# An attention and expert kernel on one core: output norms of the turn behind the sigmoid, the third G product in step 13, another order in head and tail

## What is computed

```python
qkv = x @ Wqkv + bqkv
q, k, v = split(qkv, 3)
q, k = q - mean(q), k - mean(k)
q2 = l2norm(q*q / (sum(q*q) + 1e-7), axis=channels)
k2 = l2norm(k*k / (sum(k*k) + 1e-7), axis=tokens)
kv = einsum('bnc,bnd->bcd', k2, v)
x1 = layernorm(x + (v + (q2 @ kv) / sqrt(N)) @ Wln + bln)
sel = sigmoid(x1 @ expert_sel.T)                # 16 experts
scores = relu(einsum('bsd,edh->bseh', x1, keys))
out = layernorm(x1 + einsum('bseh,ehv,bse->bsv', scores, values, sel))
```

## Time and profile before

| | us |
|---|---|
| median of 3 runs | 1004.82 |
| lowest and highest run | 1003.86 and 1009.28 |
| the profiled execution's own time | 1005.64 |
| its span in the profile | 1003.7 |
| TensorE, VectorE, ScalarE, GpSimd busy in it | 984.6, 804.1, 527.2, 54.7 |

### The profile page before, as it was taken

How to read it: one execution, slowest core, us unless ns; L and a number is a source line. 1 busy time by engine, 2 the same in 40 slices (tenths; PEclk the granted TensorE clock), 3 DMA queues, 4 the chain that set the end, 5 groups by cost and what they waited for, 6 DMA issues and landing times.

```text
span 1003.7 us, 20862 instructions
## 1 busy us (share of the span) xinstructions
PE 984.6 (98%) x7704; PEld 942.0 (94%) x7704; DVE 804.1 (80%) x1873; ACT 527.2 (53%) x1151; POOL 54.7 (5%) x75
## 2 busy tenths in 40 slices
PE   9999999999999999999999999999999999999996
PEld 8798998999999999999999999999999999999996
DVE  6799886988778887788878888788877888878545
ACT  5557535565345653556435664366644566354323
POOL 0100100001010010100101000010100101010100
PEclk9999999999999999999999999999999999999999
DMA  5152233432354223441243613325133342333221
GB/s 187 48 201 90 76 106 114 136 122 82 99 159 138 75 87 125 140 153 70 92 135 104 189 55 113 121 96 179 65 107 110 107 164 75 107 105 108 85 95 64
DMA packets 75768, 112.45 MB, mean 112 GB/s; under 512 B 7186, under 2 KB 37906, under 8 KB 75668
## 3 DMA queue, kind: packets, MB, share of 16 engines
q1 hardware_dynamic: 75668, 111.13, 33.9%
HBM read 87.51 MB, written 23.46 MB: 111 GB/s over the span
## 4 chain that ended last, share of the span: by engine, by line
PE 71%; DVE 11%; DMA 5%; issue 5%; ACT 3%; SPq 2%; POOL 0%; DVEq 0%; ACTq 0%; POOLq 0%
PE up_bank L1399 25%; PE down_bank L1399 25%; PE ring_bank L1399 9%; PE qk_bank L1399 6%; PE g_bank L1399 3%; DMA sel_all<-sel_out 3%; DVE gated_l L1137 2%; SPq L478 2%; DMA parked_x<-w_room 2%; DVE gated L1155 2%; DVE x1T_l L1001 1%; PE g_bank L1452 1%; ACT L666 1%; DMA parked_q<-w_room 1%; DVE qk L1155 1%
## 5 line engine op out<-in xcount | busy, mean ns | idle before, releaser
L1399 PE MATMUL down_bank<-vals_h,gated_h 128*128 128x256 f32 x1024 | 285.9, 279 | 1.9 <-DVE gated_l L1137 1.8
L1399 PE MATMUL down_bank<-vals_h,gated_l 128*128 128x256 f32 x1024 | 283.8, 277 | 0.0
L1399 PE MATMUL down_bank<-vals_l,gated_h 128*128 128x256 f32 x1024 | 283.8, 277 | 0.0
L1399 PE MATMUL up_bank<-x1T_h,keys_l 128*128 128x256 f32 (+1 forms) x928 | 268.6, 289 | 0.0
L1399 PE MATMUL up_bank<-x1T_l,keys_h 128*128 128x256 f32 (+1 forms) x928 | 268.6, 289 | 0.0
L1399 PE MATMUL up_bank<-x1T_h,keys_h 128*128 128x256 f32 (+1 forms) x928 | 268.5, 289 | 0.0
L598 ACT ACTIVATE gated_h<-gated 128x512 fp32r<-128x512 f32 x176 | 111.1, 631 | 198.9 <-DVE gated L1155 198.9
L1399 PEld LDWEIGHTS down_bank<-vals_h,gated_h 128*128 128x128 f32 x1024 | 192.4, 188 | 8.0 <-DVE gated_l L1137 3.6
L1399 PEld LDWEIGHTS down_bank<-vals_l,gated_h 128*128 128x128 f32 x1024 | 192.9, 188 | 4.1
L1399 PEld LDWEIGHTS down_bank<-vals_h,gated_l 128*128 128x128 f32 x1024 | 192.3, 188 | 0.0
L1155 DVE SCALAR_TENSOR_TENSOR gated<-up_bank,sel_all 128x512 f32<-128x512 f32 x176 | 121.3, 689 | 78.3 <-PE up_bank L1399 55.9
(11 more groups left out here) (276 smaller groups left out, 1772.5 us busy)
## 6 DMA issues: line engine op xcount, KB each, us to landing
sel_all<-sel_out SPq DMA_DIRECT2D x192, 256.0 KB, 3.8
x_raw<-in_x SPq DMA_DIRECT2D x15, 512.0 KB, 5.2
out<-z SPq DMA_DIRECT2D x30, 256.0 KB, 2.5
xT_raw<-in_xT SPq DMA_DIRECT2D x14, 512.0 KB, 5.3
parked_q<-w_room SPq DMA_DIRECT2D x14, 512.0 KB, 2.6
q<-parked_q SPq DMA_DIRECT2D x56, 128.0 KB, 3.0
parked_x<-w_room SPq DMA_DIRECT2D x14, 512.0 KB, 3.8
w_room<-parked_x SPq DMA_DIRECT2D x56, 128.0 KB, 3.0
```

What stands on the lines that cost most here:

```text
L1399: last = mm(dst, lhs, rhs, start=start and i == 0, stop=stop and i == n - 1, **kw)
```

## The change

In the loop:

- GG 2 (the third G product) goes from step 12 to step 13, ahead of GG 3, in the first iteration too.
- On ScalarE the sigmoid of a group (`early` of LG) goes from ahead of the copy gated_h to behind it, in every step that has one (13 and 31).
- The output norms of ZN 29 and ZN 30 are both made in step 31, behind the sigmoid (`norm_steps`); a sigmoid of one column behind z_std in step 30 takes the table load there. Their two stores go to step 31, behind `move_rows`.
- `low_is_late` is false for step 31: gated_l of step 31 is made in its own step, not behind the gate of step 0.

In the head: VectorE's `weights_lo(0)` goes ahead of the column sums, `weights_lo(1)` behind the sum of the logits; TensorE gets 4 and 3 extra fp32 matmuls of 128 columns ahead of the last x1 transposes and ahead of the logits (`keep_warm`).

In the tail: ScalarE norms one tile of each of the last two pairs, VectorE the other; ScalarE's norm stands ahead of the next z_std; each tile has its own store.

```diff
--- before.py
+++ after.py
@@ -41,7 +41,7 @@
         1: [], 2: [("ZA", 0), ("ZA", 1), ("Y", 4)], 3: [("ZN", 0), ("XS", 4)], 4: [("ZN", 1), ("Y", 5)],
         5: [("Y", 6), ("XS", 5)], 6: [("Y", 7), ("XS", 6)], 7: [("XS", 7), ("QK", 0)], 8: [("QK", 1)],
         9: [("GG", 0)], 10: [("XR", 1), ("QK", 2), ("GG", 1)], 11: [("QK", 3), ("QS", 0)],
-        12: [("GG", 2), ("QK", 4), ("LG", 1), ("QS", 1)], 13: [("GG", 3), ("QS", 2)], 14: [("QK", 5), ("QS", 3)],
+        12: [("QK", 4), ("LG", 1), ("QS", 1)], 13: [("GG", 2), ("GG", 3), ("QS", 2)], 14: [("QK", 5), ("QS", 3)],
         15: [("GG", 4), ("QK", 6), ("QS", 4)], 16: [("GG", 5), ("QS", 5)], 17: [("QK", 7)],
         18: [("ZA", 0), ("ZA", 1), ("QR", 0), ("GG", 6)], 19: [("KS", 0), ("GG", 7), ("QS", 6)], 20: [("KV", 0), ("QS", 7)],
         21: [("Y", 0)], 22: [("Y", 1), ("XS", 0)], 23: [("Y", 2), ("XS", 1)], 24: [("Y", 3), ("XS", 2)],
@@ -57,7 +57,7 @@
     0: [], 1: [], 2: [], 3: [("QT", 2)], 4: [("QT", 3)], 5: [("Y", 4)], 6: [("Y", 5)],
     7: [("Y", 6), ("XT", 4), ("QK", 0)], 8: [("Y", 7), ("XT", 5), ("QK", 1)], 9: [("XT", 6), ("GG", 0)],
     10: [("XT", 7), ("QK", 2), ("GG", 1)], 11: [("QK", 3), ("QS", 0)],
-    12: [("GG", 2), ("QK", 4), ("LG", 1), ("QS", 1)]}
+    12: [("QK", 4), ("LG", 1), ("QS", 1)]}
 FIRST = dict(LOOP, plan={**LOOP["plan"], **FIRST_PLAN}, split_xT={4: 0, 9: 1})
 LAST = dict(plan={1: [("ZA", 0), ("ZN", 0)], 2: [("ZA", 1), ("ZN", 1)]}, split_xT={}, split_x={}, bias_x={},
             gpsimd_xT=(), gpsimd_x=())
@@ -351,13 +351,17 @@
             for s in range(LAST_STEPS):
                 step(B, s)
 
+        def norm_steps(s):
+
+            return {STEPS - 2: (), STEPS - 1: (STEPS - 3, STEPS - 2)}.get(s, (s - 1,))
+
         def gate_room(s):
 
             return qk if s % 2 and s not in range(6, 19) else gated
 
         def low_is_late(it, s):
 
-            return gate_room(s) is not gate_room((s + 1) % STEPS) and (it, s) != (B - 1, STEPS - 1)
+            return gate_room(s) is not gate_room((s + 1) % STEPS) and s != STEPS - 1
 
         def last_iteration(it):
             return it == B
@@ -452,11 +456,11 @@
                 g = goff % G
                 b = it + (goff - g) // G
                 t = GT * g + 2 * p
-                if last_iteration(it) and p == 1:
-
-                    sp.wait_ge(last_out_made, 1)
+                if last_iteration(it):
+
+                    sp.wait_ge(last_out_made, p + 1)
                     sp.dma_start(out_dram[b, :, t + 1], z_room(it)[:, p, 1]).then_inc(stored[p], 16)
-                    sp.wait_ge(out_made, 2 * out_pair(it, goff, p) - 1)
+                    sp.wait_ge(out_made, 2 * out_pair(it, goff, -1) + p + 1)
                     sp.dma_start(out_dram[b, :, t], z_room(it)[:, p, 0]).then_inc(stored[p], 16)
                 else:
                     at_least(sp, out_made, 2 * out_pair(it, goff, p))
@@ -549,16 +553,17 @@
                 for kind, a, off in planned(it, s, ("LG", "ZN", "QS", "XS")):
                     if kind == "LG" and a == 0:
                         move_rows(it, off, a)
-                    elif kind == "ZN":
-                        store_pair(it, off, a)
                     elif kind in ("QS", "XS") and a % GT == GT - 1:
                         turn(it, it + off, kind, a // GT)
                 if s == ROWS_STEP and it < B:
                     move_rows(it, 0, 1)
+                for n in norm_steps(s + 1) if s < STEPS - 2 else norm_steps(s):
+                    for kind, a, off in planned(it, n, ("ZN",)):
+                        store_pair(it, off, a)
 
             run(step)
             for p in range(2):
-                sp.wait_ge(stored[p], 16 * (G * B + p))
+                sp.wait_ge(stored[p], 16 * (G * B + 1))
 
 
         @block.gpsimd
@@ -734,22 +739,34 @@
                         act.wait_ge(z_aggregated, 2 * n)
                         nc.scalar.activation(z_std[:, a], z_mv[:, a, :, 1], ACT.Sqrt,
                                              bias=eps_ln[:]).then_inc(z_rooted, 1)
-                for kind, a, off in planned(it, s - 1, ("ZN",)):
+                if s == STEPS - 2 and planned(it, s, ("LG",)):
+                    nc.scalar.activation(table_ahead[:, 1:2], eps_ln[:], ACT.Sigmoid)
+                for n in norm_steps(s):
+                    if not last_iteration(it):
+                        output_norms(it, n)
+
+            def output_norms(it, n):
+
+                for kind, a, off in planned(it, n, ("ZN",)):
                     n = out_pair(it, off, a)
                     act.wait_ge(z_shift_made, n)
-                    for i in range(1 if last_iteration(it) and a == 1 else 2):
-                        nc.scalar.activation(z_room(it)[:, a, i], z_room(it)[:, a, i], ACT.Identity, bias=z_shift[:, a, i:i + 1],
+                    for i in range(1 if last_iteration(it) else 2):
+                        nc.scalar.activation(z_room(it)[:, a, i], z_room(it)[:, a, i], ACT.Identity,
+                                             bias=z_shift[:, a, i:i + 1],
                                              scale=z_rstd[:, a, i:i + 1]).then_inc(out_made, 1)
 
             def step(it, s):
-                early(it, s, ("KS", "LG"))
+                early(it, s, ("KS",))
                 if step_exists(it, s):
                     f = step_no(it, s)
                     act.wait_ge(gate_applied, f + 1)
 
                     at_least(act, down_made, f + 1 - HELD)
                     copy(gated_h[:, f % HELD], gate_room(s)[:]).then_inc(gated_hi, 1)
+                early(it, s, ("LG",))
                 early(it, s, ("QK", "Y"))
+                if last_iteration(it):
+                    output_norms(it, s - 1)
                 late(it, s)
                 if (it, s) == (0, 0):
                     q0_squares(3)
@@ -1016,7 +1033,7 @@
                         V.scalar_tensor_tensor(out=z_shift[:, a], in0=z_mv[:, a, :, 0], scalar=-1.0,
                                                in1=z_rstd[:, a], op0=ALU.mult, op1=ALU.mult
                                                ).then_inc(z_shift_made, 1)
-                        if last_iteration(it) and a == 1:
+                        if last_iteration(it):
                             layer_norm(z_room(it)[:, a, 1], z_room(it)[:, a, 1], z_mv[:, a, 1],
                                        z_rstd[:, a, 1:2]).then_inc(last_out_made, 1)
 
@@ -1334,6 +1351,7 @@
                 dve.wait_ge(bln_in, 16)
                 V.tensor_tensor(out_bias[:], bvl[:], bln_raw, ALU.add).then_inc(out_bias_set, 1)
                 x0_bias(0)
+                weights_lo(0)
                 dve.wait_ge(cols0_summed, 1)
                 V.tensor_scalar(col_sums[:, 0:M].rearrange("p a b -> p (a b)"), cols0_place[:, 0:2 * M],
                                 EPS_NORM ** 2, None, ALU.max)
@@ -1369,12 +1387,11 @@
                     x1T_low(a)
                 for a in range(2):
                     y_finish(2 + a)
-                weights_lo(0)
                 for a in range(2):
                     x1T_low(2 + a)
-                weights_lo(1)
                 dve.wait_ge(logits_low, 1)
                 V.tensor_tensor(sel[:], logits0_bank[0:E, :], sel[:], ALU.add).then_inc(logits_summed, 1)
+                weights_lo(1)
                 for m in range(M):
                     dve.wait_ge(kv_hi, m + 1)
                     V.tensor_tensor(kvw_l[:, m], kvw0[:, m], kvw_h[:, m].bitcast(F32),
@@ -1538,6 +1555,11 @@
                         last = mm(logits0_bank[:], esel_h[:, m], x1T_l[:, 0, m], start=False,
                                   stop=(m == M - 1))
                     last.then_inc(logits_made, 1)
+
+                def keep_warm(count):
+
+                    for n in range(count):
+                        mm(down_bank[0][:, 0:P], ones[:], ident[:], start=True, stop=True)
 
                 pe.wait_ge(constants_set, 4)
                 for n in range(WARM):
@@ -1574,8 +1596,10 @@
                 x1_transpose(0)
                 x1_transpose(1)
                 queries0(2)
+                keep_warm(4)
                 x1_transpose(2)
                 x1_transpose(3)
+                keep_warm(3)
                 logits0()
 
             first_batch()
```

## The result

The changed kernel takes 1014.2 us (median; its runs lie between 1011.2 and 1019.9), against 1006.2 us of the kernel before beside it: ratio 1.0079, 95% interval [1.0052, 1.0107], slower by some 8 us. The forecast was 1009.0 with a range up to 1011.8. The profiled execution of the changed kernel is its longest, 1019.9 us of its own time and 1017.9 of span, so its difference of 14.1 us in the span is more than the typical one; about 5 us of that are a slower pace of the matmuls, told of at the end.

What follows compares the result with a forecast made beforehand. TensorE, busy 984.6 of 1003.7 us, bounds it; VectorE and ScalarE set its step-20 KV wait. 1005.6 + 6.2 - 1.9 + 0.1 - 0.4 = 1009.6; from the runs' median 1008.8, stated as 1009.0, range 1000.8 to 1011.8.

Steps and rivals of the forecast that it cites:

- Part 1: Step 13: sigmoid behind the gate's copy makes k_h 1.50 us later, then GpSimd, gate of step 17 and KV; 6.2 us lost.
- term of 6.2 us: Loss summed over seven KV products from the later gate of step 17: 5.6 plus 0.6 for colliding spreads.
- One sign: Step 20: TensorE's wait ahead of each KV product was to be 1 us.
- My last sign: Step 17: if its gate waits for GpSimd no oftener than before, Part 1 is wrong and the kernel no slower.
- Rival A: Steps 14 to 17: the spread doesn't wait for step 14's transpose, or slack absorbs 1.5 us; about 1002, chance 0.19.
- upper bound of 10.5 us: Most that Part 1 could lose, if nothing takes the delay up: 7 x 1.5 us.
- Part 2: Third G product from step 12 to 13: gain 0, at most 2 us if Part 1 costs nothing.
- Part 3: Turn of a batch: gated_l of step 31 no longer behind gate(0), so TensorE does not wait; 1.9 us gained.
- wait for z in step 2 of a turn: Turn: a small new wait for the z additions was to come next, limiting a turn's gain to 0.44 us.
- Part 4: Head: weights_lo moves and keep_warm; 2.3 us turn into new waits, 0.1 us lost (1 gained to 1.6 lost).
- Rival B: Head: new waits around the third `up` drop the clock again, costing 1.3 to 1.6 us; 1010.4, chance 0.18.
- Part 5: Tail: last store issued at 1000.4 instead of 1000.73; 0.4 us gained (0 to 0.8).

Runs made afterwards that it cites:

- e2: The kernel before with one part alone: in step 13 the sigmoid stands behind the gate's copy; ratio 1.0132.
- e3: The changed kernel with sel_rows fetched in SyncE's step 13, ahead of the parking of the q tiles, instead of step 14; ratio 1.0050 to the kernel before.
- e6: The kernel before with the turn and the tail of the change alone; ratio 0.9968.
- e7: The kernel before with the third G product moved to step 13 alone; ratio 0.9995.
- e12: The kernel before with the head of the change alone: both weights_lo moves and keep_warm; ratio 0.9995.
- e1: The changed kernel with one part undone: in step 13 the sigmoid again stands ahead of the gate's copy; ratio 0.9963 to the kernel before.
- e4: The changed kernel with the sigmoid's table loaded at the end of step 12, the sigmoid still behind the gate's copy; ratio 0.9954 to the kernel before.
- e5: The changed kernel with 128 already met waits ahead of TensorE's first matmul, 64 more instructions in its stream; ratio 1.0122 to the kernel before.

## Why the prediction was wrong, point by point

**Part 1, the step that failed.** The mechanism held up to the size: k_h 3.19 us behind the gate's start (3.22 forecast), VectorE waiting 2.27, GpSimd late for the gate of step 17 in all seven batches. The term of 6.2 us was mis-sized: e2 measures 13.3 (10.6 to 16.0), its ways 14.6. It failed in two places. One sign did not come: TensorE's waits right ahead of the seven KV products are 1.5 us together, as before, and not 1 us each, for the new waits stand earlier, at the QK product of step 14 (0.26 us in three batches) and in step 18, for x_l and z (1.8 and 2.9 us together).

First, per batch I took the spread's delay less the reserve of the gate, as if only GpSimd could be late. For the first, fourth, fifth and others that gave +1.5, +0.95, +1.05; for the third +0.83, and 1.17 came; for the second it gave 0.56, where I put 0.3 for the spreads' collision on top of 0.26, and 1.5 came. The changed kernel and e3 show that VectorE's line has less slack than the delay, too (0.75 us of it are left at gate 17 without GpSimd), so that no batch could take it up. My last sign, that the kernel is no slower if gate 17 does not wait for GpSimd, was wrong for this reason: in e3 it never waits, and e3 is slower by 0.5%. Rival A named that slack, 0.8 us in step 15, as a reason for less; it was the reason against that decided.

Second, the largest item: the fourth and sixth batch cost 7.2 us where 1.5 stood in the sum. I wrote that the parking and what follows it come "1.5 later each" and took its duration as given. In the trace of before there was already a row against this: the first batch's parking took 3.8 us, and that, not only the order of things, was why the first batch's spread was 1.2 us later against its gate than elsewhere. In the four kernels where this parking meets a block (before, e2, e6, e7) the gate of step 17 waits 1.0 to 1.4 us for GpSimd there; in e12, the kernel before with another head, it meets none and the gate doesn't wait. I used this row as the case that I expected of all; it was a collision with an instruction block. The upper bound of 10.5 us, seven times 1.5, was therefore no bound: it had no row for a DMA that gets slower by being moved, nor for a clock that falls behind waits in mid-batch. For the first batch the same error worked the other way: +1.5 forecast, +0.5 measured, for the changed kernel moved it out of its collision.

**Part 2** held, as far as e7 can tell. **Part 3** held in kind: no wait for gated_l at the turns, and 3.2 us for turn and tail together (1.1 to 5.3), where 2.3 was the sum. A wait for z in step 2 of a turn, which was to be next, is in e6 (0.41 us at 662.0); in the changed kernel all four waits for z stand in step 18.

**Part 4.** The sum was +0.1, the trace has +2.2. That weights_lo(1) would be exposed was right, 1.14 us; that the instructions behind it would run beside GpSimd's spreads was not seen and added 1.1, so that the third `up` waited 2.4 us, not 1.5. Rival B came true in this execution: the clock stood at 0.50 from 50.8 to 54.2; e1, e4 and e12 have the same wait and no fall. And the gain that was set against it, the fall at 43.9 in the earlier trace rows, was an accident of that one execution (below), so there was less to win. In the medians the head's sum is not refuted: e12 has it between 2.4 gained and 1.3 lost.

**Part 5** held in kind and gave more than its 0.4 us, and more than its bound of 0.8: the store issued last starts 3.6 us behind the start of the last z addition, 4.0 before, and from the last gate to the end it is 11.1 to 11.2 us in all ten kernels with the new tail and 12.0 to 12.1 in the four with the old one. The end comes 2.6 us behind that issue, not 3.3.

**The range.** Its top of 1011.8 was below what part 1's own upper bound gives: 10.5 for 6.2 makes 1009.0 + 4.3 = 1013.3, and with rival B's 1.4 it is 1014.7. That this lies near the measured 1014.2 is luck and no explanation, for the 13.3 us of e2 are above that bound, and turn and tail gave more than their sums.

## What to carry to other kernels

When two instructions of an engine are exchanged, look at which of them brings a table load with it: the load goes where the exchange puts it, and it may be taken ahead at no cost if the engine is idle there. Before a delay is put down to one chain, look at the slack of the parallel ones; where two are late by about as much, removing one brings little, and the work that is moved for it may lengthen the other. And a step that is moved in time meets other partners: a DMA and a vector instruction have the duration of the trace only as long as they stand beside the same things, and the bounds have to hold a row for their slow case.

## What the runs showed of the hardware

**Instruction blocks share the DMA engines with data.** In the 14 traces each 16384-byte block takes 0.9 to 2.6 us, and a parking of 512 KB that meets one while it moves its packets lands up to 2.3 us later (4.9 for 2.6), its last eight packets behind the block. Where they fall depends on the number of TensorE's instructions, for 64 more of them made the parkings of the fourth and sixth batch quick again and slowed that of the second to 4.3 us (and, less, that of the seventh to 3.2).

**The same waits, another clock.** In the head of the kernel before and of e7 TensorE waits alike. TensorE in the kernel before, then in e7:

```profile
42.90 0.50 PE L1537 MATMUL down_bank<-x1T_h,esel_hl 128*128 128x512 f32 x1 [1.36 <-DVE x1T_l L1293]
...
43.95 0.63 PE L1399 MATMUL up_bank<-x1T_h,keys_h 128*128 128x512 f32 x1
44.38 0.63 PE L1399 MATMUL up_bank<-x1T_l,keys_h 128*128 128x512 f32 x1
```

```profile
42.96 0.51 PE L1537 MATMUL down_bank<-x1T_h,esel_hl 128*128 128x512 f32 x1 [1.36 <-DVE x1T_l L1293]
...
44.01 0.39 PE L1399 MATMUL up_bank<-x1T_h,keys_h 128*128 128x512 f32 x1
44.24 0.40 PE L1399 MATMUL up_bank<-x1T_l,keys_h 128*128 128x512 f32 x1
```

In both it waited 0.91 and 1.36 us; in the one the clock fell to 1.2 GHz behind them, in the other (and in e2 and e6) it stayed at 2.4. The wait of 2.4 us for the first gate brought a fall in the changed kernel, e3 and e5, and none in e1, e4 and e12. So a fall seen once in a profile is not a sure cost, nor is its absence a sure saving.

**Two paces.** In one and the same execution the matmuls of 256 columns run at 0.113 us from start to start in most stretches and at 0.118 in others, tens of us long, with the clock granted in full. TensorE in the changed kernel, each pair of rows 36 matmuls apart, 4.24 and 4.07 us:

```profile
434.26 0.28 PE L1416 MATMUL down_bank<-vals_h,gated_h 128*128 128x256 f32 x1
...
438.50 0.28 PE L1416 MATMUL down_bank<-vals_h,gated_h 128*128 128x256 f32 x1
...
552.95 0.28 PE L1416 MATMUL down_bank<-vals_l,gated_h 128*128 128x256 f32 x1
...
557.02 0.28 PE L1416 MATMUL down_bank<-vals_l,gated_h 128*128 128x256 f32 x1
```

Summed over an execution the slower pace costs 4.8 to 11.2 us (last column of the table), and it begins and ends in different places. With one traced execution of each kernel it can't be told whether it hangs on the kernel. It is of the size of the spread between the runs of one kernel. What sets it stays open.
